# A gated delta-rule recurrence on one core: blocks inverted in place, work moved forward in TensorE's order, four matmuls fewer

## The reference

```python
def step(S, inp):
    q_t, k_t, v_t, b_g, b_beta = inp
    S = S * jnp.exp(b_g)[..., None, None]
    kv = jnp.einsum('mbhk,mbhkv->mbhv', k_t, S)
    dv = (v_t[None] - kv) * b_beta[..., None]
    S = S + k_t[..., :, None] * dv[..., None, :]
    o_t = jnp.einsum('mbhk,mbhkv->mbhv', q_t, S)
    return (S, o_t)
```

## Time and profile before

| | |
|---|---|
| Time, median of 3 runs | 4490.09 us (4484.92 to 4506.94) |
| The profiled execution's own time | 4485.37 us |
| Its span | 4483.6 us |
| PE busy | 3845.0 us (86%) |
| DVE busy | 3612.9 us (81%) |
| ACT busy | 2886.8 us (64%) |
| POOL busy | 377.9 us (8%) |
| Granted TensorE clock, mean | 0.952 |

### The profile page before, as it was taken

One profiled execution on the slowest core, in us unless ns is written; L12 is line 12 of the kernel. 1 busy time (PEld: TensorE's weight loads), 2 busy tenths in 40 slices (PEclk: granted clock), 3 DMA queues, 4 the chain that ended last, 5 costly groups with the idle time before them and its releaser, 6 DMA issues. The chain is left out here.

```text
span 4483.6 us, 194752 instructions
## 1 busy us (share of the span) xinstructions
PE 3845.0 (86%) x86225; PEld 3102.0 (69%) x86225; DVE 3612.9 (81%) x6975; ACT 2886.8 (64%) x9736; POOL 377.9 (8%) x220
## 2 busy tenths in 40 slices
PE   5511799899999998999899999999998999979999
PEld 2201677777777777777777777777777777756666
DVE  5663988888988888888888888888988888825665
ACT  5752577677766776767677666776766767644443
POOL 1130000000000000000000000000100000000000
PEclk8755899999999999999999999999999999989999
DMA  4667222322232223222322322232223222121110
GB/s 118 173 166 164 60 60 56 91 58 56 56 93 56 63 62 89 60 56 67 82 56 56 80 69 56 56 92 56 56 56 93 56 56 62 50 60 37 34 34 8
DMA packets 319915, 314.47 MB, mean 70 GB/s; under 512 B 139864, under 2 KB 252384, under 8 KB 314976
## 3 DMA queue, kind: packets, MB, share of 16 engines
q1 hardware_dynamic: 319072, 302.00, 26.6%
HBM read 232.70 MB, written 69.21 MB: 67 GB/s over the span
## 5 line engine op out<-in xcount | busy, mean ns | idle before, releaser
L911 DVE TENSOR_TENSOR run_XL<-run_XL,run_EL 128x30 f32<-128x30 f32 (+14 forms) x1920 | 637.6, 332 | 66.0
L910 DVE TENSOR_TENSOR run_EL<-run_AL,run_XL 128x30 f32<-128x30 f32 (+14 forms) x1920 | 637.1, 332 | 66.0
L978 POOL TENSOR_TENSOR run_DB<-run_DB,run_below 128x1024 f32<-128x1024 f32 x128 | 305.0, 2383 | 3310.7 <-DVE run_KP L895 1747.0
L1045 PE MATMUL run_SP<-run_KP 64*32 64x128 f32 x8192 | 552.9, 275 | 30.0 <-DVE run_KP L895 21.7
L871 DVE TENSOR_TENSOR run_SC<-run_SP,run_DB 128x512 f32<-128x512 f32 x512 | 341.2, 686 | 266.9 <-PE run_SP L1049 261.4
L794 ACT ACTIVATE run_DB<-run_DB,run_col 128x64 f32<-128x64 f32 x2048 | 548.0, 351 | 4.7 <-POOL run_DB L978 1.0
L801 ACT ACTIVATE run_KD<-run_PR,run_col 128x64 f32<-128x64 f32 x2048 | 480.3, 328 | 18.4 <-PE run_PR L1064 10.2
L854 ACT COPY run_S<-run_KS 128x256 f32<-128x256 f32 x448 | 166.7, 372 | 504.4 <-PE run_KS L1111 502.4
L1045 PEld LDWEIGHTS run_SP<-run_KP 64*32 64x32 f32 x8192 | 412.6, 107 | 99.2 <-issue 74.2
L807 ACT ACTIVATE run_R<-run_KS,run_col 128x64 f32<-128x64 f32 x1792 | 415.1, 324 | 65.5 <-PE run_KS L1072 65.3
L1007 PE MATMUL run_PR<-ident,run_win 128*64 128x128 f32 x4096 | 285.2, 282 | 169.5 <-DMA run_win<-KQ_s 153.8
(11 more groups left out here) (204 smaller groups left out, 7630.6 us busy)
## 6 DMA issues: line engine op xcount, KB each, us to landing
run_DB<-G_s SPq DMA_DIRECT2D x512, 128.0 KB, 3.0
run_EG<-EG_s SPq DMA_DIRECT2D x128, 512.0 KB, 6.9
run_tab<-TAB_s SPq DMA_DIRECT2D x128, 256.0 KB, 11.8
KQ_s<-proj_win SPq DMA_DIRECT2D x32, 768.0 KB, 7.7
run_win<-KQ_s SPq DMA_DIRECT2D x64, 384.0 KB, 3.2
TAB_s<-tab_tab SPq DMA_DIRECT2D x128, 128.0 KB, 2.4
run_V<-V_s SPq DMA_DIRECT2D x128, 128.0 KB, 3.1
V_s<-proj_vv SPq DMA_DIRECT2D x64, 128.0 KB, 3.2
```

The source lines that it names most:

```text
L910: v.link(dve.tensor_tensor(e, bcast(AL[:, r + 1:, r], 2, done), bcast(XL[:, r, 0:done], 1, rows), ALU.mult))
L911: less = dve.tensor_tensor(XL[:, r + 1:, 0:done], XL[:, r + 1:, 0:done], e, ALU.subtract)
L1045: pe.matmul(out[64 * e:64 * e + C, p].rearrange("p (z u) i -> p z (u i)", z=2), KP[f, key, p, t0:t1], KP[f, kq, p, t0:t0 + SPAN], start=Tr ...
```

## The change

Five things are done:

1. The inversion works in one tile. Before, the scores were transposed to AL, XL was made as -1 times AL with ones on the diagonal, and each round read AL and XL. Now the transpose goes to XL, the diagonal is set to -1, and each round reads XL alone. XL is then the negative of the inverse; the copies on ACT that feed XN take the factor -1, and the one to ZM loses it.
2. On PE both halves of the first merge and the first half of the second now stand ahead of the score group 3. On ACT the copies to ZM come ahead of those of the first block, and the copy of `merged(k, 1, 0)` ahead of the fourth exponential. The semaphore counts follow.
3. Score group 5 stands at the place of the second merge's other half, ahead of the first `write_state`. The groups 6 and 7, keys 0, next 0 and keys 1 follow one place earlier. On ACT the scalings keys 0 to keys 3 stand one place earlier.
4. SP waits after every two table DMAs of a new head until they have landed.
5. The four `stay_busy` matmuls are gone.

The core of the diff:

```diff
-        AL, XL, EL = sb("AL", [128, C, C]), sb("XL", [128, C, C]), sb("EL", [128, C * C // 4])
+        XL, EL = sb("XL", [128, C, C]), sb("EL", [128, C * C // 4])
...
-        PE_PLACES = [["score 4"], ["merge"], ["score 5"], ["score 6"], ["score 7"], ["keys 0"], ["next 0"], ["keys 1"],
+        PE_PLACES = [["score 4"], ["merge", "score 5"], ["score 6"], ["score 7"], ["keys 0"], ["next 0"], ["keys 1"], [],
                      ["turn 0"], ["keys 2"], ["turn 1"], ["keys 3"], ["next 1"], ["turn 2"], ["next 2"], ["turn 3"]]
-        ACT_PLACES = [["merge"], ["exp 6"], ["exp 7"], [], [], ["keys 0"], ["keys 1"], ["keys 2"],
-                      ["keys 3", "turn 0"], ["keys 4", "next 0"], ["keys 5", "turn 1"], ["keys 6", "next 1"],
+        ACT_PLACES = [["merge"], ["exp 6"], ["exp 7"], [], ["keys 0"], ["keys 1"], ["keys 2"], ["keys 3"],
+                      ["turn 0"], ["keys 4", "next 0"], ["keys 5", "turn 1"], ["keys 6", "next 1"],
...
                                 sp.dma_start(tab[at:at + HALF, k], TAB_s[h, k, e]).then_inc(l_tab, 16)
+                            if h:
+                                sp.wait_ge(l_tab, 256 * h + 64 * k + 32 * (e + 1))
...
-                    act.copy(XN[rows, :, :, 0:C], XO[rows, :, :, :]).then_inc(act_m, 1)
+                    act.activation(XN[rows, :, :, 0:C], XO[rows, :, :, :], ACT.Copy, scale=-1.0).then_inc(act_m, 1)
...
-                        act.activation(ZM[:, :, cs, 0:C], got, ACT.Copy, scale=-1.0).then_inc(act_m, 1)
+                        act.copy(ZM[:, :, cs, 0:C], got).then_inc(act_m, 1)
                     else:
-                        act.copy(XN[:, :, cs, C:], got).then_inc(act_m, 1)
+                        act.activation(XN[:, :, cs, C:], got, ACT.Copy, scale=-1.0).then_inc(act_m, 1)
...
+                        merged(k, 0, 0)
+                        merged(k, 0, 1)
                         act.wait_ge(xt_done, 2 * k + 2)
                         first_block(0)
-                        merged(k, 0, 0)
                         first_block(1)
-                        merged(k, 0, 1)
+                        merged(k, 1, 0)
                     prepare_part(k, "exp 4")
-                    if real(k):
-                        merged(k, 1, 0)
                     prepare_part(k, "exp 5")
...
-                    v.link(dve.transpose(AL[:, :, :], SC[:, n % 2, :, :, 0:C].rearrange("p a c i -> p i (a c)")))
-                    v.link(dve.tensor_scalar(XL[:, :, :], AL[:, :, :], -1.0, None, ALU.mult))
-                    v.link(dve.memset(XL[:, :, :].rearrange("p i j -> p (i j)")[:, ::C + 1], 1.0))
+                    v.link(dve.transpose(XL[:, :, :], SC[:, n % 2, :, :, 0:C].rearrange("p a c i -> p i (a c)")))
+                    v.link(dve.memset(XL[:, :, :].rearrange("p i j -> p (i j)")[:, ::C + 1], -1.0))
...
-                    v.link(dve.tensor_tensor(e, bcast(AL[:, r + 1:, r], 2, done), bcast(XL[:, r, 0:done], 1, rows), ALU.mult))
+                    v.link(dve.tensor_tensor(e, bcast(XL[:, r + 1:, r], 2, done), bcast(XL[:, r, 0:done], 1, rows), ALU.mult))
...
-                        pe.wait_ge(act_m, 6 * k + 2 + 2 * g)
+                        pe.wait_ge(act_m, 6 * k + 1 + g)
...
-                def stay_busy():
-                    pe.matmul(KS[:, 0].rearrange("p a v -> p (a v)"), ident[:, :], Sdec[:, :, :].rearrange("p a v -> p (a v)"),
-                              start=True, stop=True)
...
                     if real(k):
-                        stay_busy()
-                        stay_busy()
                         merge(k, 0, 0)
-                        stay_busy()
                         merge(k, 0, 1)
-                        stay_busy()
-                    prepare_part(k, "score 3")
                     if real(k):
                         merge(k, 1, 0)
+                    prepare_part(k, "score 3")
```

## The result

The changed kernel takes 4421.83 us (median of 4 runs, 4410.63 to 4432.15), the kernel before 4487.51 us beside it (4 runs). The ratio is 0.9857, with an interval of 0.9836 to 0.9878: 1.4% faster. The profiled execution took 4432.15 us, with a span of 4430.4. The forecast was 4425 us.

A forecast was written before the change was run, and what follows sets the result against it. TensorE's written order was taken to set the step. The sum was 4485.4 - 220 - 3 - 33 - 19 + 214 = 4424, stated as 4425 us; own range 4340 to 4510, overall range 4235 to 4600.

The forecast's parts named there:

- order: Key rows and score group 5 earlier: two TensorE waits of 0.76 us a step go, 0.3 us given back.
- blocks: In-place inversion on VectorE: the 1.12 us multiply by -1 goes, paying only because TensorE got shorter.
- four matmuls out, with the clock: Unread matmuls around the merges: 2.32 us a step saved on TensorE, but 214 us lost to falls to 1.2 GHz.
- table limit: Two tables at a time at seven head changes: TensorE's issue stops go, 12 of 45 us remain, -33 us.
- The bound: TensorE in its written order sets the step; VectorE follows with about 3 us to spare.
- The queue's length: TensorE's step shrinks by 3.55 us to 50.44 us at full clock.
- The clock: Small merge matmuls in a row, 4.3 us, make TensorE fall to 1.2 GHz in most steps; chance 0.50.
- lapse of 0.4 us: A 0.38 us gap in TensorE's second merge preceded one fall; such a lapse there was taken as enough.
- The price of a fall: Each fall costs 4.6 us, in three steps of four: 62 x 0.75 x 4.6 = 214 us.
- The tables: At each head, eight pairs take 4.1 us each, 33 in all, plus 3 behind EG: 6 us late for VectorE.
- PE has about 6 us of cover: At late tables TensorE has about 6 us cover at score groups, leaving 2 to 4 us a head.
- Blocks as cover: Without in-place blocks VectorE would set the step at 51.2 us, 0.7 us a step more.

The follow-up runs named there:

- e6: The kernel before with only the moves in the order of TensorE and ScalarE (score group, key rows, merges ahead); 4415.8 us, ratio 0.9870.
- e5: The kernel before with only the in-place blocks (one tile for the elimination, signs moved into ScalarE's copies); 4475.4 us, ratio 0.9999.
- e9: The changed kernel without the table limit and with the four unread matmuls put back; 4416.6 us, ratio 0.9863 to the kernel before.
- e2: The changed kernel with the four unread matmuls put back around the merges, table limit kept; 4429.8 us, ratio 0.9893 to the kernel before.
- e1: The changed kernel without SyncE's wait after each pair of table transfers; 4389.4 us, ratio 0.9793 to the kernel before.
- e4: The kernel before with only the wait after each pair of table transfers added; 4503.2 us, ratio 1.0046.
- e3: The kernel before with only the four unread matmuls taken out; 4489.2 us, ratio 1.0019.
- e11: The changed kernel without the table limit, a step's last eight output matmuls moved between the next step's second and third merge; 4357.6 us, ratio 0.9724.
- e7: The changed kernel without the table limit, with six extra VectorE scratch fills once before the first elimination; 4392.3 us, ratio 0.9817 to the kernel before.
- e8: The changed kernel with six extra VectorE scratch fills once before the first elimination; 4410.2 us, ratio 0.9857 to the kernel before.
- e10: The changed kernel without the table limit, each table transfer cut in two by token, first halves sent earlier; 4364.5 us, ratio 0.9748.

## Why the prediction was right, and where only its sum was

Forecast 4425, measured 4422, faster as said. By parts, 62 steps each:

| term | predicted us | measured us | from |
|---|---|---|---|
| order | -76 | -58 | e6 |
| blocks | 0 alone | 0 | e5; -3, e6 to e9 |
| four matmuls out, with the clock | -144 + 214 - 19 = +51 | -16 to -31 | e2 to changed, e9 to e1 |
| table limit | -33 | +13 to +29 | e2 and e9, changed and e1 |

Along either way from before to the changed kernel they sum to the measured 0.9857, -64 us, as differences of the ratios must: -58 - 3 - 31 + 29 over e6, e9, e1, or -58 - 3 + 13 - 16 over e6, e9, e2. Two terms were off by 46 to 82 us in opposite directions, so the sum was right by luck. The forecast's own signs say the same. It called itself wrong if a drop cost other than 4 to 5 us, or if steps at full clock were not near 50.4 us: the first came true, the second in part.

**The bound** was right. TensorE's written order sets the step and VectorE follows with slack: e5 shows it, and so do the waits.

**The queue's length** was right. Predicted was 50.44 us in a step at full clock. In the changed kernel from first merge to first merge:

```profile
3760.10 2.21 PE L1030 MATMUL run_PR<-run_TM,run_SC 32*32 32x32 f32 x128
...
3810.76 2.21 PE L1030 MATMUL run_PR<-run_TM,run_SC 32*32 32x32 f32 x128
```

50.66 us, and in it one stop of 0.51 us inside the merges. It is the shorter of the two steps at full clock; the other took 51.5, and eight such in e1 50.8 in the median. Between two XO, where the prediction looked for 50 to 51 us, the two at full clock took 51.8 and 52.6. That they carry what TensorE was late by before is argued, not shown.

**The clock** was right in kind. "I therefore expect the fall to 1.2 GHz in most steps": 60 of 62 have time at half clock, 57 have a fall of their own, and the mean in the stage is 0.94. Behind it the Trainium skill's page "TensorE: Matmul & The Clock Gate", section "Why this matters for your kernels", asks for no long idle gaps; by that rule the clock stays up in this stage. The trace does not agree: 3.15 of 3.15 us busy ahead of the fall, and 27 more falls like it. The prediction's "lapse of 0.4 us" is not needed either.

**The price of a fall** is the term that was mis-sized. "The value is 4.6 us, near the measured one": the measured one, the step of 58.85 us, had a fall of 10.2 us. More than half of the new ones are 3.4 us long, and of the 45 ordinary steps with low clock 5 took the 55 to 58 us that were to show it; their mean is 53.6. 5.5 us at half in a step at 0.38 us each are 2.1 us, where 0.75 x 4.6 = 3.45 was put. What I should have read off is how long the low clock lasted in that one step, and priced by the microsecond, not by the fall. And the stops inside the merges, 22.0 us in all, were not foreseen.

**The tables** are the step that failed. "Two tables are 0.5 MB, so I expect the stops gone": the long ones did go. "4.1 us, in all 33 ... So 6 us late": the eight pairs took 39.7 to 44.0 us, and VectorE waited 10.1 to 13.5 us. Seven pairs of eight took 4.6 us each in the mean, near what was put. The first took 9.5, where 3 and 4.1 were put: it is issued while EG's two transfers of 512 KB are on their way, which land 6.4 to 7.9 us later. "PE has about 6 us of cover": that was near. VectorE stood 80.4 us for tables and TensorE behind it 23.0 + 11.7 = 34.7, so 6.5 us a head were covered and 5.0 were not. The working's own "2 to 4 us remain on each head" is 14 to 28 us, where it then took 12. And TM came late to TensorE at all seven heads, with low clock behind it (7 to 14 us at half behind each head, up to 23.7 in e4). The seven head steps stand 55 us above the ordinary ones (7 x 7.8), where 12 were predicted.

**Smaller slips.** Of the fifteen stops before, thirteen lie beside tables, not fourteen, and a fifth fall lies outside the table loads, at 2682 us behind a stop of 2.7 us. The high end of the tables' lateness is 28 us by its own terms (6.9 x 8 + 3 - 30.3), not 25. The chances add up to 0.08 for the same time and 0.30 for a slower one, not 0.09 and 0.29.

**Blocks as cover.** That without them VectorE would set 51.2 us and cost 0.7 a step was not tested: no kernel here has the old blocks together with the new order and the four out.

## What to carry to other kernels

A transfer that crowds the queues should be sent earlier in pieces, as soon as a piece of its tile is free; a limit on how many are in flight makes the last one late, and a late transfer can be paid again in the clock of the engine that waited (e4). Work that nobody reads can earn its time by keeping the clock up, as in the old order (e3), and stop earning it when the order changes (e9 to e1). Real work moved in among small matmuls gave the faster kernel here (e11), for a reason that is not settled. When two terms of opposite sign carry a forecast, measure each alone before believing the sum.

## What the runs showed of the hardware

- TensorE's clock fell to 1.2 GHz 28 times right behind 3.15 us in which its records have no gap, most of them in 32 x 32 and 32 x 64 matmuls (1039.20 to 1042.35: 3.15 of 3.15 us), and 20 times in the same place of the step with some gap ahead (changed kernel). In e9, with the four wide matmuls back, the falls there are 22, 21 of them without a gap. Four 128 x 128 matmuls of 256 columns around them cut the time at half clock from 5.5 to 1.2 us a step (e2).
- Behind an idle gap of 2.2 us before the merges it ran 23.7 us at half clock, busy 23.61 of them (e4).
- Late in 192 small matmuls come stops of 0.3 to 2.0 us with nothing to wait for: 25 in e1, one in e9 with the four long matmuls between, 25 in e3 (to 3750 us) with a score group between but the four out. They are tied to a place in the program, not to a time: in the changed kernel, e1, e7, e8 and e10 the stop of a given step stands behind the same number of merge matmuls (155 in pass 9, 165 in pass 13, 175 in pass 17). From one fourth step to the next it stands ten further on (135, 145, 155, ... 185), as a boundary in the stream of instructions would. The Trainium skill's page "Runtime: NRT & Kernel Launch", "Instruction fetch mechanics", calls the fetching of instructions mostly hidden; if these stops are that, it is not so for matmuls this short. That they are fetches no row says.
- Two transfers of 256 KB alone land in 4.0 us and allow a pair every 5.1 us (changed kernel); sixteen at once land in a median of 11.8 us but were all there in time (kernel before). The first pair, beside two transfers of 512 KB, took 9.5 us.
